# Routed expert results added to the output in DRAM by accumulating scatters

## The chip, the cores and the metric

The kernel runs on one core of a Trainium2 chip. A core has TensorE (PE, matrix products), VectorE (DVE), ScalarE (ACT), GpSimd (POOL) and SyncE (SP). Each has its own instruction queue, and they meet by semaphores. TensorE writes PSUM, here eight banks of 128 x 512 float32. DMA queues of SP, ACT and POOL feed the core's 16 DMA engines; the indirect ones, with a row index for each partition, are issued by GpSimd. The metric is the device time of one execution in microseconds (us), the median of several runs.

## What is computed

Eight blocks of 128 tokens, 512 wide, go through two layers with gated residuals. The change touches the last step alone, a mixture of experts added to x:

```python
# x = x + tanh(g_ffn[1]) * moe(layernorm(x))
logits = xt @ router_w + router_b
scores = softmax(logits) + router_bias
g = scores.reshape(T, GROUPS, E // GROUPS)              # 16 experts, 4 groups
_, gidx = top_k(g.max(axis=-1), LIM)                    # the 2 best groups
masked = where(keep[:, :, None], g, -inf).reshape(T, E)
_, idx = top_k(masked, K)                               # the 2 best experts
gate = zeros((T, E)).at[arange(T)[:, None], idx].add(vals)
for w1, b1, w2, b2, w3, b3, ge in experts:              # INTER = 128
    h = silu(xt @ w1 + b1) * (xt @ w2 + b2)
    y = y + ge[:, None] * (h @ w3 + b3)
z = silu(xt @ sw1 + sb1) * (xt @ sw2 + sb2) @ sw3 + sb3 # shared, 2 x 128
return y + z
```

T is 1024. Each token has two routed experts (TOP = 2), so there are 2048 token-expert pairs.

## The kernel before

The long part of the kernel, the two attention steps and the first feed-forward step, up to about 1100 us, is left as it is. Behind it come three pieces.

**The router and the shared experts.** VectorE works out the choice in many small steps (`router_shift`, `router_groups`, `router_choice`). TensorE multiplies the shared experts' weights in four pieces (`inner_part(n, 0)` and `(n, 1)`, n = 0 to 3; n = 0 and 1 are the first four token blocks, 2 and 3 the last four). Each piece then goes through ScalarE (`silu_of`), VectorE (`hidden`), ScalarE (`hidden_high`, the high half of a split float32) and GpSimd (`hidden_low`, the low half). `outer(t)` multiplies block t by the output weights, 7 matmuls into bank 4 or 5. ScalarE copies it out with the gate (`shared_rows`), GpSimd adds it to `x_sb` (`add_shared`), and from the third block on `outer` waits until the bank two blocks back has been copied.

**The sorting.** `rank_tokens` counts, by products with the 0/1 choice `chosen_b`, how many tokens go to each expert and which rank each has. VectorE turns this into tiles of 128 rows of one expert (`tile_ranges`, `places`): 31 tiles (TILES) hold the 2048 pairs, with empty places. `turn_selection` transposes the map from tiles to experts (`sel`, taken over into `sel_t`). `gather_tokens` gives every place its token number (`token_i`) by 16 products, and `load_offset` reads the address of each tile's weights.

**The loop over 31 tiles.** GpSimd gathers the tile's 128 token rows from DRAM (`gather(j)`, 256 KB, four buffers). TensorE transposes them (`turn_x_rows`), multiplies by w1 and w2 (`routed_inner`), transposes the hidden rows (`turn_hidden`) and multiplies by w3 (`routed_outer`, into bank 6 or 7). ScalarE copies the result to `y_rows`, two buffers (`take_y`), and SP stores it in `y_dram`. When all 31 are stored, GpSimd gathers 16 times 128 rows from `y_dram` back in token order (`y_back`), VectorE multiplies each by its gate and adds it to `x_sb` (`add_routed`), and SP stores the eight blocks of `out`.

The order on every queue is the order in which the functions are called in the code. In TensorE's loop it is

```python
for j in range(TILES):
    if j + 1 < TILES:
        routed_inner(j + 1)
    turn_hidden(j)
    if j + 2 < TILES:
        turn_x_rows(j + 2)
    routed_outer(j)
```

Of the kernel before, what the change touches and what calls it, by code (L numbers as in the profile page):

```python
# [18 lines left out]
F32 = mybir.dt.float32  # L19
# [35 lines left out]
def build(nc, x, ctx, ctx_t, g_xattn, g_ffn, wq, wkv, wo, q_w, k_w, w_gate, w_up, w_down, router_w, router_b,  # L55
          router_bias, s_w, s_b12, r_w, e_b, rows_dram, y_dram, out):
    with ExitStack() as top:
# [26 lines left out]
        slot_gates = sb("slot_gates", [P, TOP * NB])  # L84
        pos_row = sb("pos_row", [P, P])
# [8 lines left out]
        sel_t = sb("sel_t", [P, TL + 2], F32R)  # L94
        offset_i = sb("offset_i", [1, TL], I32)
        token_i = sb("token_i", [P, TL], U32)
        slot_i = sb("slot_i", [P, TOP * NB], U32)
# [68 lines left out]
        at[0] = gu_at - 2 * EW * 4  # L166
        y_back = put("y_back", [P, TOP * NB, D])
# [18 lines left out]
        at[0] = stage_at  # L186
        x_rows = put("x_rows", [P, 4, D])
        x_cols = put("x_cols", [P, 2, KC, P])
# [30 lines left out]
        dest, dest_tile, dest_pos = (put(n, [P, TOP * NB]) for n in ("dest", "dest_tile", "dest_pos"))  # L219
# [66 lines left out]
        y_loaded = [sem(f"y_loaded{i}") for i in range(PAIRS)]  # L286
        r_added = sem("r_added")
# [88 lines left out]

        block = top.enter_context(nc.Block())
# [3 lines left out]
        def _(sp):  # L381
# [103 lines left out]
        def _(pool):  # L485
# [6 lines left out]
            def routing_maps():  # L492
# [6 lines left out]
                          allow_small_or_imprecise_dtypes=True).then_inc(maps_ready, 1)  # L499
                pool.memset(ones_b[:, :], 1.0).then_inc(maps_ready, 1)  # L500
                pool.memset(chosen_b[:, NB, :], 0.0).then_inc(maps_ready, 1)
                pool.memset(tri[:, :, :], 1.0).then_inc(maps_ready, 1)
                pool.memset(sel[:, :], 0.0).then_inc(maps_ready, 1)
                pool.wait_ge(maps_ready, 7)
# [4 lines left out]
                for i, col in enumerate((E, 32 + E)):  # L509
                    pool.affine_select(out=sel[:, :], in_=sel[:, :], compare_op=ALU.not_equal, fill=1.0,  # L510
                                       base=-64 * TL - col, pattern=[[1, P]], channel_multiplier=64)\
                        .then_inc(maps_ready, 1)
                    pool.wait_ge(maps_ready, 10 + i)
# [181 lines left out]
        def _(act):  # L695
# [289 lines left out]
        def _(dve):  # L985
# [250 lines left out]
            chunks(dve, inner_chunk)  # L1236
            dve.wait_ge(bias_high, 1)
# [112 lines left out]
            def router_groups():  # L1350
# [7 lines left out]
                dve.wait_ge(maps_ready, 11)  # L1358
# [35 lines left out]
            def places():  # L1394
# [27 lines left out]
                dve.tensor_copy(slot_i[:, :], dest[:, :]).then_inc(places_ready, 1)  # L1422

            def take_selection():
                dve.wait_ge(sel_turned, 1)
                dve.tensor_copy(sel_t[:, :], bank[7][:, 0:TL + 2]).then_inc(sel_copied, 1)
# [7 lines left out]
            def gate_slots():  # L1434
# [5 lines left out]
                                       ALU.add))  # L1440

# [20 lines left out]
            def add_routed(c, t):  # L1462
                n = TOP * t + c
                dve.wait_ge(y_loaded[t // 2], 16 * 2 * TOP)
                dve.wait_ge(r_added, n) if c else dve.wait_ge(e_added, t + 1)
                dve.scalar_tensor_tensor(out=x_sb[:, t, :], in0=y_back[:, c * NB + t, :],
                                         scalar=slot_gates[:, c * NB + t:c * NB + t + 1], in1=x_sb[:, t, :],
                                         op0=ALU.mult, op1=ALU.add).then_inc(r_added, 1)


# [13 lines left out]
            gate_slots()  # L1484
            routed_hidden(0)
# [4 lines left out]
            for t in range(NB):  # L1490
                for c in range(TOP):
                    add_routed(c, t)
# [497 lines left out]
```

## Time and profile before

| | |
|---|---|
| median of 3 runs | 1299.7 us (1299.63 to 1300.89) |
| the profiled execution | 1297.4 us, its span 1295.2 us |
| busy, share of the span | PE 92%, DVE 63%, ACT 44%, POOL 26% |
| granted clock of TensorE | 0.975 of 2.4 GHz in the mean |

The span goes from the first to the last instruction of the core. Busy shares are means over stages with different limits: TensorE is busy nearly all the time until the routed loop ends, and idle behind it. A chain of waits follows the work that ended last back to what released it, step by step. "issue" in it is time in which the engine waited for nothing that the profile shows. A DMA's time "to landing" counts from the start of the instruction that issues it to its completion.

### The profile page before, as it was taken

What the parts mean: (1) busy time and instruction counts of PE and PEld (TensorE: products, weight loads), DVE (VectorE), ACT (ScalarE), POOL (GpSimd) and SP (SyncE); (2) the same over time, 40 slices, a digit from 0 to 9 for tenths busy, and PEclk for the clock granted to TensorE, in tenths of its full rate; (3) what the DMA queues carried; (4) which work ended last, traced back from release to release, by engine and by line L of the source; (5) the groups of instructions that cost most, each with busy time, mean ns of one, the idle gap of its engine ahead of it and who ended that gap; (6) DMA issues with size and microseconds to landing.
All of it is one profiled execution on the core that took longest, in us unless ns stands there. A gap on an engine that the chain in (4) does not pass through costs nothing.

```text
span 1295.2 us, 20292 instructions
## 1 busy us (share of the span) xinstructions
PE 1196.3 (92%) x6771; PEld 1015.7 (78%) x6771; DVE 818.3 (63%) x2402; ACT 575.4 (44%) x1345; POOL 340.7 (26%) x283
## 2 busy tenths in 40 slices
PE   5899999999999999999999999979999887899990
PEld 5788898888888888898889888857877664677760
DVE  6767667667666766766766766676878687611113
ACT  3545455454455454554555545433444323233430
POOL 4413023122121221321302312213432133252205
PEclk9999999999999999999999999989999998899995
DMA  7001001000000100100100000102213138134436
GB/s 260 1 34 49 2 34 50 1 32 16 32 32 2 47 32 0 49 0 32 49 0 32 0 1 1 52 1 77 65 57 100 65 98 320 70 113 138 141 109 199
DMA packets 39557, 77.41 MB, mean 60 GB/s; under 512 B 5266, under 2 KB 21650, under 8 KB 37460
## 3 DMA queue, kind: packets, MB, share of 16 engines
q1 hardware_dynamic: 34596, 62.36, 14.1%
q0 software_dynamic: 3760, 12.32, 3.6%
q10 hardware_dynamic: 1152, 2.10, 0.4%
q8 instruction: 28, 0.46, 0.2%
q14 instruction: 21, 0.17, 0.0%
HBM read 64.45 MB, written 12.32 MB: 59 GB/s over the span
## 4 chain that ended last, share of the span: by engine, by line
PE 54%; DVE 23%; issue 10%; ACT 6%; POOL 5%; DMA 1%; SPq 1%; DVEq 0%; POOLq 0%; ACTq 0%
PE bank L330 13%; PE bank L332 12%; PE bank L331 12%; PE bank L1838 4%; DVE iq L1232 2%; ACT probs L755 2%; PE bank L1586 2%; PE bank L1856 2%; DVE probs L1089 2%; DVE k_junk L1046 2%; PE bank L1722 2%; DVE row_max L1062 1%; DVE pt_lo L1076 1%; POOL k_rstd L540 1%; PE bank L1533 1%
## 5 line engine op out<-in xcount | busy, mean ns | idle before, releaser
L755 ACT ACTIVATE probs<-bank,exp_bias,q_rstd 128x256 f32<-128x256 f32 x256 | 141.2, 562 | 142.8 <-DVE exp_bias L1070 142.8
L1081 DVE TENSOR_TENSOR o_lo<-bank,o_hi 128x512 fp32r<-128x512 f32 x64 | 44.2, 691 | 186.3 <-ACT o_hi L748 186.2
L330 PE MATMUL bank<-wkv_hi,kv_src_lo 128*128 128x256 f32 x512 | 146.2, 286 | 3.0 <-POOL wkv_lo L522 3.0
L332 PE MATMUL bank<-wkv_hi,kv_src_hi 128*128 128x256 f32 x512 | 146.0, 285 | 0.0
L331 PE MATMUL bank<-wkv_lo,kv_src_hi 128*128 128x256 f32 x512 | 145.8, 285 | 0.0
L544 POOL TENSOR_TENSOR q_rstd<-q_var,minus_half 128x8 f32<-128x8 f32 x32 | 52.4, 1638 | 304.3 <-DVE q_var L1049 304.3
L744 ACT ACTIVATE pt_hi<-bank 128x512 fp32r<-128x512 f32 x128 | 69.7, 597 | 115.9 <-PE bank L1586 115.9
L330 PE MATMUL bank<-wo_hi,o_lo 128*128 128x512 f32 x256 | 105.4, 412 | 1.0 <-DVE o_lo L1081 1.0
L330 PE MATMUL bank<-wq_hi,kv_src_lo 128*128 128x512 f32 x256 | 103.2, 403 | 0.0
L330 PEld LDWEIGHTS bank<-wkv_hi,kv_src_lo 128*128 128x128 f32 x512 | 98.6, 193 | 4.7 <-issue 3.4
L332 PE MATMUL bank<-wo_hi,o_hi 128*128 128x512 f32 x256 | 102.1, 399 | 0.0
L331 PE MATMUL bank<-wo_lo,o_hi 128*128 128x512 f32 x256 | 101.9, 398 | 0.0
L332 PE MATMUL bank<-wq_hi,kv_src_hi 128*128 128x512 f32 x256 | 100.6, 393 | 0.0
L331 PE MATMUL bank<-wq_lo,kv_src_hi 128*128 128x512 f32 x256 | 100.3, 392 | 0.0
L331 PEld LDWEIGHTS bank<-wkv_lo,kv_src_hi 128*128 128x128 f32 x512 | 98.7, 193 | 1.4
L332 PEld LDWEIGHTS bank<-wkv_hi,kv_src_hi 128*128 128x128 f32 x512 | 98.7, 193 | 0.0
L540 POOL TENSOR_TENSOR k_rstd<-k_var,minus_half 128x4 f32<-128x4 f32 x32 | 32.5, 1016 | 248.6 <-DVE k_var L1023 248.6
L1062 DVE TENSOR_REDUCE row_max<-bank 128x2 f32<-128x512 f32 x128 | 84.7, 684 | 18.4 <-PE bank L332 17.6
L1089 DVE TENSOR_SCALAR probs<-probs,row_inv 128x256 f32<-128x256 f32 x256 | 88.0, 407 | 2.2
L330 PE MATMUL bank<-k_hi,q_lo 128*128 128x256 f32 x256 | 78.3, 306 | 6.6 <-DVE q_lo L1055 5.4
L1076 DVE TENSOR_TENSOR pt_lo<-bank,pt_hi 128x512 fp32r<-128x512 f32 x128 | 81.7, 679 | 0.0
L331 PE MATMUL bank<-k_lo,q_hi 128*128 128x256 f32 x256 | 73.1, 286 | 0.0
(256 smaller groups left out, 3089.2 us busy)
## 6 DMA issues: line engine op xcount, KB each, us to landing
weights<-r_w SPq DMA_DIRECT2D x16, 768.0 KB, 8.8
wq_raw<-wq SPq DMA_DIRECT2D x8, 1024.0 KB, 4.8
wo_raw<-wo SPq DMA_DIRECT2D x8, 1024.0 KB, 4.8
y_dram<-y_rows SPq DMA_DIRECT2D x31, 256.0 KB
wkv_raw<-wkv SPq DMA_DIRECT2D x8, 512.0 KB, 3.3
gu_raw<-w_gate SPq DMA_DIRECT2D x10, 256.0 KB, 3.3
gu_raw<-w_up SPq DMA_DIRECT2D x10, 256.0 KB, 3.7
wd_raw<-w_down SPq DMA_DIRECT2D x10, 256.0 KB, 4.0
```

Source lines behind the costliest of these rows:

```text
L330: eng.matmul(out_ap, a_lo, b_hi, start=start, stop=False)
L331: eng.matmul(out_ap, a_hi, b_lo, start=False, stop=False)
L332: return eng.matmul(out_ap, a_hi, b_hi, start=False, stop=stop)
L540: pool.tensor_tensor(k_rstd[:, :], k_var[:, :], minus_half[:, 0:4], ALU.pow).then_inc(k_rstd_ready, 1)
L544: pool.tensor_tensor(q_rstd[:, par, :], q_var[:, :], minus_half[:, 0:2 * R], ALU.pow)\
L744: act.activation(pt_hi[:, c, :], pt_ps[c][:, :], ACT.Copy).then_inc(pt_hi_ready, 1)
L755: act.activation(probs[:, h, :], scores_ps[h // 2][:, (h % 2) * 256:(h % 2) * 256 + 256], ACT.Exp, bias=exp_bias[:, h:h + 1], scale=q_rstd ...
L1062: dve.tensor_reduce(row_max[:, 2 * half:2 * half + 2], scores_ps[half][:, :].rearrange("p (h n) -> p h n", h=2), AX.X, ALU.max)\
L1076: dve.tensor_tensor(pt_lo[:, c, :], pt_ps[c][:, :], pt_hi[:, c, :].bitcast(F32), ALU.subtract)\
L1081: dve.tensor_tensor(o_lo[:, par, :], o_ps[:, :], o_hi[:, par, :].bitcast(F32), ALU.subtract)\
L1089: dve.tensor_scalar(probs[:, h, :], probs[:, h, :], row_inv[:, h:h + 1], None, ALU.mult)\
L1838: mm = pe.matmul(bank[j % 2][:, 0:2 * P], x_cols[:, j % 2, k, :], weights[:, bass.ds(at_weights[j] + k * 2 * P, 2 * P)], start=False, stop ...
```

## The change

`y_dram`, `y_back`, `slot_i`, the 16 gathers and the 16 adds are gone. Instead:

- SP stores block t of `out` as soon as the shared part has been added to it. A ninth block is stored too; it takes the rows of empty places, and is cut off on the host.
- `take_y` scales each result row by the gate of its place (`place_gates`).
- GpSimd adds the tile's 128 rows to the rows of `out` in DRAM by an indirect DMA with `compute_op=ADD` (`scatter(j)`), once the nine stores have landed. Each scatter waits until the one before has landed. The gathers from tile 4 on are issued in between.
- The output row and the gate of each place (`place_i`, `place_gates`) come from 16 further products (`gather_late`) of 96 columns, prepared by VectorE (`gate_slots`) and taken over by `take_late`.
- The bias selector of the shared part is a tensor of its own (`shared_sel`), so `outer` needs no `sel_t`. `outer(0)` to `outer(3)` move ahead of `rank_tokens`; `outer(6)` and `outer(7)` move between the offset loads and the loop. ScalarE's and GpSimd's queues are reordered to match.
- `x_rows` and `x_cols` move to the start of the shared memory region, where `xt_hi` was.

```diff
@@ sync @@
-            for j in range(TILES):
-                sp.wait_ge(y_rows_ready, j + 1)
-                sp.dma_start(y_dram[j * P:j * P + P, :], y_rows[:, j % 2, :]).then_inc(y_stored[j % 2], 16)
             for t in range(NB):
-                sp.wait_ge(r_added, TOP * (t + 1))
+                sp.wait_ge(e_added, t + 1)
                 sp.dma_start(out[t, :, :], x_sb[:, t, :]).then_inc(stored, 16)
-            sp.wait_ge(stored, 16 * NB)
+            sp.dma_start(out[NB, :, :], x_sb[:, 0, :]).then_inc(stored, 16)
+            sp.wait_ge(stored, 16 * (NB + 1))
+            for i in range(2):
+                sp.wait_ge(y_stored[i], 16 * ((TILES + 1 - i) // 2))
@@ gpsimd @@
-            add_shared(0)
-            add_shared(1)
+            for t in range(4):
+                add_shared(t)
             hidden_low(3)
-            add_shared(2)
-            add_shared(3)
             pool.wait_ge(tokens_ready, 1)
...
+            def scatter(j):
+                pool.wait_ge(y_rows_ready, j + 1)
+                if j >= 1:
+                    pool.wait_ge(y_stored[(j - 1) % 2], 16 * ((j + 1) // 2))
+                pool.indirect_dma_start(out_rows, bass.IndirectOffsetOnAxis(ap=place_i[:, j:j + 1], axis=0),
+                                        y_rows[:, j % 2, :], None, compute_op=ALU.add).then_inc(y_stored[j % 2], 16)
+
             for j in range(4):
                 gather(j)
             for t in range(4, NB):
                 add_shared(t)
-            for j in range(4, TILES):
-                pool.wait_ge(x_rows_turned, j - 3)
-                gather(j)
-            for i in range(2):
-                pool.wait_ge(y_stored[i], 16 * ((TILES + 1 - i) // 2))
-            for t in range(NB):
-                for c in range(TOP):
-                    q = c * NB + t
-                    pool.indirect_dma_start(y_back[:, q, :], None, y_dram[:, :],
-                                            bass.IndirectOffsetOnAxis(ap=slot_i[:, q:q + 1], axis=0))\
-                        .then_inc(y_loaded[t // 2], 16)
+            pool.wait_ge(late_taken, 2)
+            pool.wait_ge(stored, 16 * (NB + 1))
+            for j in range(TILES):
+                if j + 4 < TILES:
+                    pool.wait_ge(x_rows_turned, j + 1)
+                    gather(j + 4)
+                scatter(j)
@@ scalar @@
-            shared_rows(0)
-            shared_rows(1)
+            for t in range(4):
+                shared_rows(t)
             silu_of(3)
             hidden_high(3)
-            for t in range(2, NB):
+            for t in range(4, NB - 1):
                 shared_rows(t)
...
                     act.wait_ge(e_added, NB)
-                act.activation(y_rows[:, j % 2, :], bank[6 + j % 2][:, :], ACT.Copy).then_inc(y_rows_ready, 1)
+                    act.wait_ge(late_taken, 2)
+                act.activation(y_rows[:, j % 2, :], bank[6 + j % 2][:, :], ACT.Copy, scale=place_gates[:, j:j + 1])\
+                   .then_inc(y_rows_ready, 1)
 
             take_x_cols(0)
+            shared_rows(NB - 1)
             take_x_cols(1)
@@ vector @@
-                dve.tensor_copy(slot_i[:, :], dest[:, :]).then_inc(places_ready, 1)
...
+                step(dve.tensor_copy(gates_hi[:, :], slot_gates[:, :]))
+                step(dve.tensor_tensor(gates_lo[:, :], slot_gates[:, :], gates_hi[:, :].bitcast(F32), ALU.subtract))
...
+                for i, value in enumerate((place[:, :], gates_hi[:, :].bitcast(F32), gates_lo[:, :].bitcast(F32))):
+                    dve.tensor_tensor(at_late[:, :, i * TL:i * TL + TL], at_tile[:, :, :],
+                                      value.unsqueeze(2).broadcast_to([P, TOP * NB, TL]), ALU.mult).then_inc(late_ready, 1)
...
-            for t in range(NB):
-                for c in range(TOP):
-                    add_routed(c, t)
@@ tensor @@
+            def gather_late():
+
+                pe.wait_ge(late_ready, 3)
+                for q in range(TOP * NB):
+                    mm = pe.matmul(bank[7][:, 128:128 + 3 * TL], at_pos[:, q, :], at_late[:, q, :], start=(q == 0),
+                                   stop=(q == TOP * NB - 1))
+                mm.then_inc(late_done, 1)
...
+            pe.wait_ge(shared_sel_ready, 1)
+            for t in range(4):
+                outer(t)
             rank_tokens()
             inner_part(3, 0)
             inner_part(3, 1)
             turn_selection()
-            pe.wait_ge(sel_copied, 1)
-            outer(0)
-            outer(1)
-            outer(2)
-            outer(3)
             gather_tokens()
-            for t in range(4, NB):
-                outer(t)
+            outer(4)
+            outer(5)
             pe.wait_ge(offset_ready, 1)
...
+            outer(6)
+            turn_x_rows(0)
+            outer(7)
+            gather_late()
+            turn_x_rows(1)
             pe.wait_ge(weights_loaded, 16 * E)
-            turn_x_rows(0)
-            turn_x_rows(1)
             routed_inner(0)
```

GpSimd's queue, the end of it, before: the shared additions, the gathers of the loop, then those behind it.

```order
L660 TENSOR_TENSOR x_sb<-s_rows,x_sb 128x512 [waits e_rows_ready] x2
L673 DMA x_rows<-rows_dram,token_i 128x512 [waits rows_stored1,rows_stored0,tokens_ready]
L673 DMA x_rows<-rows_dram,token_i 128x512 x3
L660 TENSOR_TENSOR x_sb<-s_rows,x_sb 128x512 [waits e_rows_ready] x4
L673 DMA x_rows<-rows_dram,token_i 128x512 [waits x_rows_turned] x27
L689 DMA y_back<-y_dram,slot_i 128x512 [waits y_stored1,y_stored0]
L689 DMA y_back<-y_dram,slot_i 128x512 x15
```

And now:

```order
L667 TENSOR_TENSOR h_lo<-e_h,h_hi 128x512 [waits h_hi_ready]
L683 DMA x_rows<-rows_dram,token_i 128x512 [waits rows_stored1,rows_stored0,tokens_ready]
L683 DMA x_rows<-rows_dram,token_i 128x512 x3
L672 TENSOR_TENSOR x_sb<-s_rows,x_sb 128x512 [waits e_rows_ready] x4
L683 DMA x_rows<-rows_dram,token_i 128x512 [waits x_rows_turned,stored,late_taken]
L691 DMA out<-y_rows,place_i 1152x512 [waits y_rows_ready]
L683 DMA x_rows<-rows_dram,token_i 128x512 [waits x_rows_turned]
L691 DMA out<-y_rows,place_i 1152x512 [waits y_stored0,y_rows_ready]
```

The last two rows repeat, with `y_stored1` and `y_stored0` in turn: a gather stands ahead of each scatter, 27 of them, and the last four scatters follow one another. The gather of tile 4 now stands behind the wait for the nine stores.

TensorE's queue around the rank product (operands `chosen_b`), before: the end of the third inner piece, the rank product, the start of the fourth inner piece.

```order
L332 MATMUL bank<-xt_hi,e_hi 128x512
L1795 MATMUL bank<-chosen_b,before_t 128x144 [waits chosen_ready,bias_split,logits_ready]
L1798 MATMUL bank<-chosen_b,ones_b 128x128
L1798 MATMUL bank<-chosen_b,ones_b 128x112
L1798 MATMUL bank<-chosen_b,ones_b 128x96
```

And now, from the end of the third inner piece, with the rows of `outer(0)` and then the end of `outer(3)`:

```order
L339 MATMUL bank<-xt_hi,e_hi 128x512
L337 MATMUL bank<-e_hi,h_lo 128x512 [waits e_lo_ready,shared_sel_ready,h_lo_ready,bias_split,logits_ready]
L338 MATMUL bank<-e_lo,h_hi 128x512
L339 MATMUL bank<-e_hi,h_hi 128x512
...
L1813 MATMUL bank<-bias_t,shared_sel 128x512
L1820 MATMUL bank<-chosen_b,before_t 128x144 [waits chosen_ready]
L1823 MATMUL bank<-chosen_b,ones_b 128x128
```

Four outer products, 28 matmuls, have moved from behind the transposed selection to ahead of the rank product.

## Rows read from the trace of the kernel before

**Rows 1.** The page: the span.

```profile
span 1295.2 us, 20292 instructions
```

**Rows 2.** Windows by stage: length, busy time (instructions) of each engine, clock, DMA share, GB/s.

```profile
core 0: us, PE busy (x) PEld busy (x) DVE busy (x) ACT busy (x) POOL busy (x), PEclk, DMA share, GB/s
1112.90:1117.80 4.90, 0.04 (x2) 0.06 (x2) 4.49 (x14) 1.97 (x3) 1.26 (x1) 0.92 0.00 0
1117.80:1123.60 5.80, 5.80 (x21) 4.70 (x22) 4.55 (x15) 0.63 (x1) 1.52 (x1) 0.50 0.00 0
...
1146.30:1261.00 114.70, 113.93 (x519) 83.49 (x519) 15.31 (x62) 44.28 (x91) 26.69 (x28) 1.00 0.42 130
```

**Rows 3.** Chain of waits, one tile: start us, us, what.

```profile
1150.24 0.11 PE bank L1848
...
1153.93 0.11 PE bank L1848
```

**Rows 4.** Chain of waits, after the last tile.

```profile
1261.07 0.61 ACT y_rows L971
...
1261.69 2.03 DMA y_dram<-y_rows
1263.71 0.26 issue
1263.97 0.95 POOL y_back L689
1264.92 0.30 issue
...
1283.94 5.62 DMA y_back<-y_dram,slot_i
...
1291.96 0.75 DVE x_sb L1466
```

**Rows 5.** Tile x_rows, gathers of the loop: duration ns min/median/max, time to landing.

```profile
L673 POOL DMA_INDIRECT x_rows<-rows_dram,token_i x25: 945/947/957, 1151.1 to 1239.7; - x25
...
DMA to landing us min/median/max: 3.5/4.2/4.8
```

**Rows 6.** Tile y_back, the gathers behind the loop.

```profile
DMA to landing us min/median/max: 3.4/4.1/5.6
```

**Rows 7.** Tile out, plain stores of 256 KB.

```profile
DMA to landing us min/median/max: 2.0/3.7/4.4
```

**Rows 8.** DMA queues, 1264 to 1290 us: packets, MB, share of 16 engines.

```profile
q0 software_dynamic: 1280, 4.20, 58.0%
```

**Rows 9.** Timeline of GpSimd (POOL): start us, us, instruction, idle time before it.

```profile
1112.98 1.26 POOL L655 TENSOR_TENSOR h_lo<-e_h,h_hi 128x512 fp32r<-128x512 f32 x1 [9.07 <-ACT h_hi L885]
...
1137.50 1.20 POOL L673 DMA_INDIRECT x_rows<-rows_dram,token_i  x1 [0.18 <-issue]
...
1147.56 0.97 POOL L673 DMA_INDIRECT x_rows<-rows_dram,token_i  x1 [0.16 <-issue]
```

**Rows 10.** Timeline of TensorE (PE).

```profile
1117.77 0.28 PE L1795 MATMUL bank<-chosen_b,before_t 128*128 128x144 bf16 x1 [4.86 <-DVE chosen_b L1376]
...
1127.20 0.50 PE L330 MATMUL bank<-e_hi,h_lo 128*128 128x512 f32 x1 [0.35 <-DVE sel_t L1426]
...
1133.75 1.85 PE L1814 MATMUL bank<-at_token,at_pos 128*128 128x32 f32 x16
```

**Rows 11.** Timeline of ScalarE (ACT).

```profile
1118.32 0.63 ACT L885 ACTIVATE h_hi<-e_h 128x512 fp32r<-128x512 f32 x1 [3.42 <-DVE e_h L1446]
...
1152.13 0.60 ACT L971 ACTIVATE y_rows<-bank 128x512 f32<-128x512 f32 x1 [0.71 <-issue]
```

**Rows 12.** Timeline of VectorE (DVE).

```profile
1126.95 0.19 DVE L1426 CAST sel_t<-bank 128x34 fp32r<-128x34 f32 x1 [3.94 <-PE bank L1805]
...
1130.82 1.27 DVE L1422 CAST slot_i<-dest 128x16 uint32<-128x16 f32 x1
...
1135.64 0.19 DVE L1430 CAST token_i<-bank 128x32 uint32<-128x32 f32 x1 [2.85 <-PE bank L1814]
```

More of the change, by code:

```diff
@@ L55, in build @@
 def build(nc, x, ctx, ctx_t, g_xattn, g_ffn, wq, wkv, wo, q_w, k_w, w_gate, w_up, w_down, router_w, router_b,
-          router_bias, s_w, s_b12, r_w, e_b, rows_dram, y_dram, out):
+          router_bias, s_w, s_b12, r_w, e_b, rows_dram, out):
     with ExitStack() as top:
@@ L165, in build @@
         weights = put("weights", [P, E * EW])
-        at[0] = gu_at - 2 * EW * 4
-        y_back = put("y_back", [P, TOP * NB, D])
+        at[0] = start
+        x_rows = put("x_rows", [P, 4, D])
+        x_cols = put("x_cols", [P, 2, KC, P])
+        at_late = put("at_late", [P, TOP * NB, 3 * TL], F32R)
         at[0] = stage_at
@@ L218, in build @@
         tiles_before = put("tiles_before", [P, E, E])
-        dest, dest_tile, dest_pos = (put(n, [P, TOP * NB]) for n in ("dest", "dest_tile", "dest_pos"))
+        dest, dest_tile, dest_pos, place = (put(n, [P, TOP * NB]) for n in ("dest", "dest_tile", "dest_pos", "place"))
         at[0] = e_h_at
@@ L285, in build @@
         y_stored = [sem(f"y_stored{i}") for i in range(2)]
-        y_loaded = [sem(f"y_loaded{i}") for i in range(PAIRS)]
-        r_added = sem("r_added")
+        late_ready, late_done, late_taken = sem("late_ready"), sem("late_done"), sem("late_taken")
+        shared_sel_ready = sem("shared_sel_ready")
         gu_hi_ready = sem("gu_hi_ready")
@@ L375, in chunks @@
             one_chunk(CH - 1, 0, TAIL, 0)
+        out_rows = out.rearrange("a p n -> (a p) n")
         block = top.enter_context(nc.Block())
@@ L508, in routing_maps @@
                                    pattern=[[1, E], [-1, E]], channel_multiplier=0).then_inc(maps_ready, 1)
[L509 to L513, printed above, removed]
+                for i, row in enumerate((E, 32 + E)):
+                    pool.affine_select(out=shared_f[:, :], in_=shared_f[:, :], compare_op=ALU.not_equal, fill=1.0,
+                                       base=-row, pattern=[[0, 1]], channel_multiplier=1).then_inc(maps_ready, 1)
+                    pool.wait_ge(maps_ready, 13 + i)
             def ln_root(i, s=0):
@@ L1440, in gate_slots, with take_late @@
                                        ALU.add))
+                step(dve.tensor_copy(gates_hi[:, :], slot_gates[:, :]))
+                step(dve.tensor_tensor(gates_lo[:, :], slot_gates[:, :], gates_hi[:, :].bitcast(F32), ALU.subtract))
+                step(dve.scalar_tensor_tensor(out=place[:, :].rearrange("p (c t) -> p c t", c=TOP),
+                                              in0=dest_pos[:, :].rearrange("p (c t) -> p c t", c=TOP), scalar=-1.0,
+                                              in1=token_less[:, :].unsqueeze(1).broadcast_to([P, TOP, NB]), op0=ALU.mult,
+                                              op1=ALU.add))
+                dve.wait_ge(h_done, 4 * SHARED)
+                for i, value in enumerate((place[:, :], gates_hi[:, :].bitcast(F32), gates_lo[:, :].bitcast(F32))):
+                    dve.tensor_tensor(at_late[:, :, i * TL:i * TL + TL], at_tile[:, :, :],
+                                      value.unsqueeze(2).broadcast_to([P, TOP * NB, TL]), ALU.mult).then_inc(late_ready, 1)
+            def take_late():
+                dve.wait_ge(late_done, 1)
+                dve.tensor_scalar(place_i[:, :], bank[7][:, 128:128 + TL], past_rows[:, 0:1], None, ALU.add)\
+                    .then_inc(late_taken, 1)
+                dve.tensor_copy(gates_taken[:, :], bank[7][:, 128 + TL:128 + 2 * TL]).then_inc(late_ready, 1)
+                dve.wait_ge(late_ready, 4)
+                dve.tensor_tensor(place_gates[:, :], bank[7][:, 128 + 2 * TL:128 + 3 * TL], gates_taken[:, :], ALU.add)\
+                    .then_inc(late_taken, 1)
             def hidden(n):
@@ L1804, in turn_selection @@
                 pe.wait_ge(sel_ready, 2)
-                pe.transpose(bank[7][:, 0:TL + 2], sel[0:TL + 2, :], ident[0:TL + 2, 0:TL + 2])\
+                pe.transpose(bank[7][:, 0:TL], sel[0:TL, :], ident[0:TL, 0:TL])\
                     .then_inc(sel_turned, 1)
@@ L1983 @@
             for k, v in arrays.items()}
-    out = nc.dram_tensor("out", (NB, P, D), F32, kind="ExternalOutput").ap()
+    out = nc.dram_tensor("out", (NB + 1, P, D), F32, kind="ExternalOutput").ap()
     rows_dram = nc.dram_tensor("rows_dram", (NB * P, D), F32, kind="Internal").ap()
-    y_dram = nc.dram_tensor("y_dram", (TILES * P, D), F32, kind="Internal").ap()
-    build(nc, rows_dram=rows_dram, y_dram=y_dram, out=out, **args)
+    build(nc, rows_dram=rows_dram, out=out, **args)
     r = run_bass_kernel_spmd(nc, [arrays], core_ids=[0])
-    return r.results[0]["out"]
+    return r.results[0]["out"][:NB]
```

40 lines of the change are left out of this document (24 added, 16 removed).

## The prediction

> **What bounds the kernel now.** I read four views. First the page for the span, 1295.2 us [rows 1]. Then the windows and the chain of waits of the routed stage. From 1146.3 to 1261.0 TensorE is busy 113.93 of 114.70 us at the full clock of 2.4 GHz [rows 2], and one tile's step follows the next after 3.69 us (1150.24 to 1153.93) [rows 3], so this loop of 31 tiles is bound by TensorE. Third the chain behind it [rows 4]: the last y_rows copy ends at 1261.68, its store lands 2.03 us later, GpSimd wakes 0.26 us after that, issues 16 gathers one behind the other (0.95 us each with 0.30 between most of them), the last one lands 5.62 us after its start, and VectorE's last add ends at 1292.71. The store that follows takes 2.0 us [rows 7] and the span ends 0.5 us behind it. So 33.5 us lie behind the last copy, in which TensorE does nothing. Fourth, the timelines ahead of the loop, for the moved outer products.
>
> **What the change takes away.** The whole tail: the last store to y_dram, 16 gathers, 16 adds and 8 stores of out. With the tail gone and nothing put in its place the span would end near 1262.
>
> **What it adds, the term that decides.** Each tile's 128 result rows are now added to the output in DRAM by an accumulating scatter from GpSimd's queue, and scatter j waits until scatter j-1 has landed. Neither y_rows (two buffers) nor PSUM (two banks) lets TensorE run more than a few tiles ahead. So if a scatter's cycle S is longer than TensorE's 3.69 us, the loop runs at S, and the scatters are the chain. S = wake of GpSimd + L, where L is the time from the start of the scatter's issue to its landing. The wake is 0.26 us [rows 4]. No row shows an accumulating DMA, so L is bounded from rows.
>
> - Below: the quickest gather of the same 128 rows of 2 KB by the same queue landed 3.4 us after its start [rows 6]. The scatter also reads 128 scattered rows from DRAM, and writes to DRAM too, so I find no reason for less.
> - Above: a gather of the loop, 4.2 us at the median [rows 5], followed by a whole store of 256 KB, 2.0 us at the least [rows 7], the two not overlapping: 6.2 us.
> - Taken: the loop's gather, 4.2 us, which has its issue of 0.95 us in it and shares the engines with one other transfer per tile, as the scatter will (the gather of tile j+5 takes the place of the y_dram store). To it comes the moving of a second 256 KB, since the destination rows and the rows of y_rows are both read. What one gather occupies is 58.0% of 26 us over 16 gathers = 0.94 us [rows 8]. L = 4.2 + 0.94 = 5.14 us and S = 5.40 us. This is nearer to the middle than to an end; I keep both ends.
>
> In the trace a gather moves its bytes once, and 0.94 us is that share. The Trainium skill, Collectives: The Full Stack, section The bandwidth ceiling, says that a reducing transfer is slower because it needs two source reads on one read ring, and not because of the addition. No run here shows it; by that rule the second 0.94 us is right and the sum stands, and without it L would be 4.2 us and the sum 1296.
>
> The gather of tile j+5 is issued inside the flight of scatter j: 0.95 us of issue [rows 5] out of L less the scatter's own issue, about 4.2 us, so it costs nothing as long as L is over 2.5 us. The scaling by the gate rides on the copy that was there (0.60 us [rows 11]) and costs nothing.
>
> **Where the first scatter starts.** It needs y_rows of tile 0, written until 1152.73 [rows 11], and all nine stores of out. The pieces ahead of the loop, one by one:
>
> - Outer products 0 to 3 move ahead of the rank product. That product waited 4.86 us for VectorE's choice and began at 1117.77 [rows 10]. Four outer products took 1127.20 to 1133.75, 6.55 us, or 1.6 each [rows 10]. Outer 0 can begin when the low half of block 1 is there, 1112.98 + 1.26 = 1114.24 [rows 9], and outer 1 ends at 1117.5. But outer 2 waits until ScalarE has emptied bank 4, and ScalarE does that only behind the copy of 1118.32 to 1118.95 [rows 11], plus 0.69: 1119.6. Outer 3 ends at 1122.9. So the rank product, with VectorE's tile ranges and places queued behind it, is late by about 5.1 us.
> - It gets back part: before, the clock fell to 1.2 GHz behind the idle 4.9 us, 0.50 from 1117.8 to 1123.6 [rows 2]. If it does not fall, the 5.8 us at the half level become 2.9. The transposed selection then comes at about 1126.95 - 0.2 + 5.1 - 2.9 = 1129. From there to the last at_pos was 1130.9 - 1126.95 = 4.0 us, and the 1.27 us cast to slot_i behind it is gone [rows 12]: 1133. TensorE has nothing to do in between, so gather_tokens ends right behind, about 1134.4, not at 1135.6, and token_i comes about 1 us earlier than 1135.64 [rows 12]. The first gather moves from 1137.50 [rows 9] to about 1136.5.
> - That 1 us is spent again: outer 7 (1.6 us) and 16 small products for the late places (1.85 us for the 16 like them [rows 10], perhaps a little more with 96 columns in place of 32) now stand between the two transposes of x_rows. Routed work begins at about 1146.3 as before, give or take 1.5 us. VectorE's new casts and products (some 3 us) end near 1140, under outer products.
> - The nine stores of out: the last shared add ends near 1146.5 and a store lands in 2.0 to 4.4 us [rows 7], so by 1151. Queued behind that wait on GpSimd is the gather of tile 4, which left at 1147.56 [rows 9]; leaving at 1151 it lands at 1155.2, and its transpose is due three steps after 1146.3 + 3.9, near 1157.5. Covered; without that cover it would cost the difference once.
>
> So the first scatter starts at 1152.73 + 0.26 = 1153.0.
>
> **The sum.** Last landing = 1153.0 + 31 S - 0.26; the span ends 0.5 us later: 1153.2 + 31 x 5.40 = 1320.6. Against 1295.2 this is +25.4 us: the loop's 31 tiles cost 31 x (5.40 - 3.69) = 53.0 us more, the tail of 33.5 us shrinks to the last scatter's 5.9. The profiled execution took 1297.4 us, so 1322.8 for it; the median of the runs, 1299.7, is 2.3 above that, and 1299.7 + 25.4 = 1325.
>
> **The point of balance.** The span stays at 1295.2 when S = (1295.2 - 1153.2) / 31 = 4.58, that is L = 4.32 us. The median gather, 4.2, is just below it. Everything hangs on how much an accumulating scatter takes more than a gather.
>
> **Rivals.**
>
> 1. Faster: the second read and the write overlap the first, row by row. For it speaks that a plain store lands in 2.0 us [rows 7], so writing to DRAM has no long receipt, and that quiet gathers took 3.4. At L = 4.2 the sum is 1291.5, or 1296 by the median; at L = 3.4, S is 3.66, TensorE bounds the loop, and the span ends at 1261.7 + 0.26 + 3.4 + 0.5 = 1265.8, 29.4 less: 1270. Against it: the same bytes can't be moved twice in the time of once, and the loop's gathers were at 4.2 and not 3.4 because of their neighbour. It decides below L = 4.24. Chance 0.15. Part of it is a page's rule: the Trainium skill, DMA: Bandwidth & Descriptors, section Anatomy of one DMA, gives 2.0 us plus bytes over 436 GB/s for a DMA of this queue, an estimate of 2.6 us for 256 KB. TensorE would bound the loop by that rule too, at 1270; the trace's quickest gather, 3.4 us, disagrees, and I give that end 0.03 of the 0.15.
> 2. No change: L between 4.24 and 4.41, by chance. 0.05.
> 3. Dearer: read, add and write of a row stand one behind another, or the issue is longer for the added descriptors. At L = 6.2 the sum is 1153.2 + 31 x 6.46 = 1353.5, or 1358; beyond that 0.07.
> 4. The clock: TensorE is busy 3.69 of 5.40 us, and it fell to the half level once behind 4.9 us of idling [rows 2]. If it stayed low, a tile would need up to 2 x 3.69 = 7.4 us and TensorE would bound the loop: 1153.2 + 31 x 7.4 = 1382.6, or 1387. Against it: idle pieces here are 1.7 us, and when it is the bound it is busy throughout, in which state the clock came back within 5.8 us [rows 2]. 0.03.
>
> **How the numbers follow.** The forecast, L from 4.41 to 6.2 (1302 to 1358), has 0.70. Faster by over 0.2% (2.6 us, about what can be told from no change here) 0.15, same 0.05, slower 0.80. The range goes from 1290 (L = 4.0, a little of rival 1) to 1360 and leaves out about 0.2.
>
> **What would show it.** Right: scatters follow each other at 5.4 us, each gap on GpSimd ended by the previous scatter's landing, landing 5.1 us after issue; TensorE's share in the loop near 0.7; the rank product 3 to 6 us later, the first y_rows within 1.5 us of 1152.7; the end one landing behind the last scatter. Wrong: a pace of 3.7 us with TensorE full, a landing under 4.3 us, or a granted clock near 0.5 in the loop.

## Result and the profile after

The changed kernel takes 1334.6 us in the median of 4 runs (1334.1 to 1336.0) against 1299.9 us before, a ratio of 1.0269 with a 95% interval of 1.0255 to 1.0283. Timed a second time beside the experiments below it stood at 1.0256 (1.0232 to 1.0279). The profiled execution took 1334.5 us, its span 1332.8 us. The forecast was 1325 us, slower, in a range of 1290 to 1360 us.

The windows of the loop and its end, with the columns of [rows 2]:

```profile
core 0: us, PE busy (x) PEld busy (x) DVE busy (x) ACT busy (x) POOL busy (x), PEclk, DMA share, GB/s
...
1200.00:1250.00 50.00, 36.70 (x147) 25.91 (x146) 4.47 (x16) 12.36 (x26) 21.82 (x18) 0.90 0.53 95
...
1310.00:1333.00 23.00, 3.04 (x8) 1.11 (x7) 0.87 (x3) 2.23 (x4) 6.25 (x4) 0.64 0.34 46
```

TensorE was busy 113.93 of 114.70 us in the loop before [rows 2]; now it is busy 36.70 of 50, a share of 0.73. The chain of waits over the first scatters (start us, us, what) is a chain of landings, where [rows 3] was one of matrix products:

```profile
1158.65 4.90 DMA out<-y_rows,place_i
...
1163.60 0.75 issue
1164.35 4.77 DMA out<-y_rows,place_i
1169.16 0.05 issue
1169.20 0.70 ACT y_rows L985
1169.91 4.95 DMA out<-y_rows,place_i
...
1174.95 0.70 ACT y_rows L985
...
1175.78 4.69 DMA out<-y_rows,place_i
```

The instructions of the tile `out` (duration ns min/median/max, first and last start us, then the time to landing) and of the gathers in the same loop, to be set beside [rows 5, 6]:

```profile
L691 POOL DMA_INDIRECT out<-y_rows,place_i x31: 1550/1587/1643, 1158.7 to 1327.7; - x31
...
DMA to landing us min/median/max: 4.4/4.8/5.7
```

```profile
L683 POOL DMA_INDIRECT x_rows<-rows_dram,token_i x27: 963/990/1004, 1155.5 to 1301.9; - x27
...
DMA to landing us min/median/max: 3.4/4.4/4.8
```

From the first start, 1158.65, to the last, 1327.66, the 30 cycles take 5.63 us each. A scatter lands 4.8 us after its start; the other 0.8 us is GpSimd's way from that landing to the next start. The gathers' own issue is nearly unchanged, 0.99 us, and a scatter's is 1.59 us.

One reading needs care. The timeline of GpSimd names ScalarE's copy as what released most scatters:

```profile
1164.35 1.59 POOL L691 DMA_INDIRECT out<-y_rows,place_i  x1 [2.75 <-DMA out<-y_rows,place_i]
...
1169.91 1.58 POOL L691 DMA_INDIRECT out<-y_rows,place_i  x1 [2.68 <-ACT y_rows L985]
...
1175.78 1.60 POOL L691 DMA_INDIRECT out<-y_rows,place_i  x1 [2.99 <-ACT y_rows L985]
```

```profile
1165.07 0.69 ACT L985 ACTIVATE y_rows<-bank,place_gates 128x512 f32<-128x512 f32 x1 [0.71 <-PE bank L1891]
...
1169.20 0.69 ACT L985 ACTIVATE y_rows<-bank,place_gates 128x512 f32<-128x512 f32 x1 [1.15 <-DMA out<-y_rows,place_i]
```

The scatter at 1169.91 sends the third tile's rows, which were copied from 1165.07 on and had been ready since 1165.8. The copy at 1169.20 is the fourth tile's; it was itself released by the landing at 1169.1 of the scatter that used its buffer. Both hang on the same landing, and the profile names the one that ended later. The chain's "0.70 ACT y_rows" between two landings is therefore not a price of ScalarE; the first pair, 1163.56 to 1164.35 (the 0.75 us of issue), shows the same gap with no copy in it. From the second scatter on, each one's rows had been copied 2.3 us or more before it started.

### The profile page after: what moved, and what is told of

It reads as the page before. It is cut to its first block, busy times and chain, and to the rows that moved or that the text cites. A ratio compares the mean times of both kernels' runs of the same rounds, so it can differ in the third digit from the quotient of the medians.

```text
span 1332.8 us, 20323 instructions
## 1 busy us (share of the span) xinstructions
PE 1212.3 (91%) x6787; PEld 1024.8 (77%) x6787; DVE 811.7 (61%) x2395; ACT 575.9 (43%) x1345; POOL 374.1 (28%) x301
## 4 chain that ended last, share of the span: by engine, by line
PE 46%; DVE 22%; DMA 12%; issue 10%; ACT 7%; POOL 3%; SPq 1%; DVEq 0%; POOLq 0%; ACTq 0%
PE bank L337 13%; PE bank L339 13%; PE bank L338 12%; DMA out<-y_rows,place_i 11%; DVE iq L1248 2%; ACT probs L768 2%; PE bank L1611 2%; DVE probs L1105 2%; DVE k_junk L1062 2%; PE bank L1747 2%; ACT y_rows L985 1%; DVE row_max L1078 1%; DVE pt_lo L1092 1%; POOL k_rstd L552 1%; PE bank L1558 1%
## 5 line engine op out<-in xcount | busy, mean ns | idle before, releaser
L552 POOL TENSOR_TENSOR k_rstd<-k_var,minus_half 128x4 f32<-128x4 f32 x32 | 32.5, 1016 | 247.9 <-DVE k_var L1039 247.9
L1496 DVE COPY g_ht<-bank 128x128 f32<-128x128 f32 x31 | 9.0, 292 | 119.2 <-PE bank L1881 119.2
```

The lines of the kernel that those rows point to most:

```text
L552: pool.tensor_tensor(k_rstd[:, :], k_var[:, :], minus_half[:, 0:4], ALU.pow).then_inc(k_rstd_ready, 1)
```

## Experiments

Each rests on the profile of one execution unless an interval stands beside it. The second trace of the kernel before belongs first, since it says which differences between two traces mean anything.

**The kernel before once more.**

> The kernel before, unchanged, for a second trace. The changed kernel's choice (chosen_b) came 4.0 us later than in the first trace of before, and in its variants 1.9 to 4.6 us later. If that is spread between executions, this trace has its choice anywhere from 1117 to 1122 us and its span moves with it, 1293 to 1299 us. If it is the change (rival), it stands at 1117.3 us within 0.5 again.

Its span and its choice, and below them the choice in the changed kernel:

```profile
span 1299.0 us, 20292 instructions
```

```profile
1121.77 0.29 DVE L1376 TENSOR_TENSOR chosen_b<-r_pick 128x128 bf16<-128x128 f32 x1
```

```profile
1121.36 0.29 DVE L1394 TENSOR_TENSOR chosen_b<-r_pick 128x128 bf16<-128x128 f32 x1
```

The same kernel has its choice at 1121.77, 4.4 us later than in the first trace (1117.3), and a span of 1299.0 in place of 1295.2 us. The changed kernel stands at 1121.36. The second trace of the changed kernel has it at 1119.6. So the 4.0 us by which all of the changed kernel's routed part is late against the first trace lie within the spread between executions of one kernel, and need no cause in the change. Seven timed executions of the kernel before went from 1298.5 to 1302.6 us. From here on I count from the choice. That leaves a smaller spread: the first y_rows copy starts 34.8 us after the choice in the first trace of the kernel before and 35.4 us after it in the second.

**The addition left out.**

```diff
-  y_rows[:, j % 2, :], None, compute_op=ALU.add).then_inc(y_stored[j % 2], 16)
+  y_rows[:, j % 2, :], None).then_inc(y_stored[j % 2], 16)
```

> The scatters write the rows instead of adding them (the addition into the output is left out), still one at a time. Theory A: the addition is paid where the scatter is issued (1.59 us of issue against 0.95 for a gather, and a longer start-up ahead of it, 0.77 against 0.3), so without it issue falls to about 0.95 us, landing to 3.0 to 3.4 us, the cycle goes under 3.7 us, TensorE bounds the loop again and the span is about 1273 us. Rival B: it is the indexed write to DRAM that is dear and the addition is free in the stream: issue stays near 1.6 us, the cycle at 5.2 to 5.6 us, the span at 1320 to 1333 us.

```profile
span 1271.4 us, 20323 instructions
```

```profile
L691 POOL DMA_INDIRECT out<-y_rows,place_i x31: 969/987/1009, 1156.6 to 1267.9; - x31
```

```profile
1264.27 2.69 DMA out<-y_rows,place_i
...
1266.99 0.02 POOLq L690
1267.01 0.70 issue
```

```profile
core 0: us, PE busy (x) PEld busy (x) DVE busy (x) ACT busy (x) POOL busy (x), PEclk, DMA share, GB/s
...
1190.00:1260.00 70.00, 70.00 (x323) 51.19 (x322) 9.26 (x38) 29.49 (x57) 35.29 (x36) 1.00 0.42 139
```

The same 31 indexed writes, one at a time, issue in 0.99 us and land 2.7 us after their start, and TensorE is busy 70.00 of 70 us again. The trace shows a landing only where a scatter waited for it, six times; five were at 2.7 to 2.8 us and one at 3.8. The time is 1273.1 us, the span 1271.4 against 1332.8. Theory A holds for the cost as a whole: index and DRAM are cheap, the addition (with its read of the old row, which no run takes apart from it) is what costs, 0.6 us of it at issue and 1.5 us (3.2 less 1.7 us behind the issue) in flight. Its second half falls: the 0.7 us and more between a landing and the next start is there for the plain scatter too, 0.79 to 1.09 us in those six starts (the last from 1266.97 to 1267.93). The other scatters started 0.27 us and more after ScalarE's copy.

**Half the columns, and half the rows.**

```diff
-  pool.indirect_dma_start(out_rows, ...place_i[:, j:j + 1]..., y_rows[:, j % 2, :], ...
+  pool.indirect_dma_start(half, ...place_i[:, j:j + 1]..., y_rows[:, j % 2, 0:D // 2], ...   # e2
+  pool.indirect_dma_start(out_rows, ...place_i[0:P // 2, j:j + 1]..., y_rows[0:P // 2, j % 2, :], ...   # e7
```

> The scatters add only the first 256 of 512 columns, into a DRAM buffer of their own (the other half of each row is left out), 128 rows each as before. Prediction's term (the second read moves its bytes in 0.94 us, so half the bytes save about 0.9 us of both reads): landing falls from 4.8 to about 3.9 us, cycle to 4.7 us, span near 1305 us. Theory A (issue by rows, flight mostly latency): issue stays at 1.59 us, landing 4.4 to 4.7 us, cycle 5.2 to 5.5 us, span 1319 to 1330 us.

> The scatters add only the first 64 of the 128 rows of each tile, all 512 columns (the other rows are left out). Half the bytes, as with half the columns, and half the rows. If the issue goes by rows: issue falls from 1.59 to 0.9 to 1.1 us and landing to 3.1 to 3.4 us (3.8 less the saved issue), cycle about 4.1 us, span 1285 to 1292 us. If the issue is a fixed cost of adding: issue stays at 1.59, landing 3.8 us as with half the columns, cycle 4.65 us, span near 1304 us.

The first run writes to a DRAM buffer of its own, with nine more stores ahead of the first scatter, which so starts late (1161.3). Rows of the first, then of the second:

```profile
L693 POOL DMA_INDIRECT half<-y_rows,place_i x31: 1549/1586/1644, 1161.3 to 1298.8; - x31
...
DMA to landing us min/median/max: 3.5/3.8/4.1
```

```profile
L691 POOL DMA_INDIRECT out<-y_rows,place_i x31: 1405/1441/1502, 1158.3 to 1293.8; - x31
...
DMA to landing us min/median/max: 3.4/3.7/4.8
```

Half the bytes take 1.0 to 1.1 us off the landing, in both shapes: 3.8 and 3.7 in place of 4.8 us. The prediction's term holds (half the bytes were to save 0.9 us), and its number for the first run, landing 3.9 and span 1305, met 3.8 and 1303.4. The issue hardly goes by rows, 1.44 us for 64 and 1.59 for 128; with a cycle of 4.52 us and a span of 1298.2 the half rows lie nearer to a fixed issue (4.65 us) than to one by rows (4.1 us), and match neither. An estimate, if the bytes count in proportion, takes an accumulating scatter of 256 KB apart: 1.59 us issue, some 1.2 us that depend on nothing tried here, and 2.0 us for the bytes, where 0.94 us was a gather's share [rows 8].

**Nothing beside the scatters.**

```diff
             for j in range(TILES):
-                if j + 4 < TILES:
-                    pool.wait_ge(x_rows_turned, j + 1)
-                    gather(j + 4)
                 scatter(j)
```

> As the changed kernel, but the gathers from tile 4 on are left out (the tiles reuse the first four tiles' rows), so that no other transfer runs beside a scatter. Prediction's step (0.7 to 0.8 us of the 4.2 us gather was its neighbour, 3.4 without one): landing falls from 4.8 to 4.0 to 4.2 us, cycle from 5.63 to 4.9 us, span near 1311 us. Rival (the scatter's time is its own): landing 4.7 to 4.8 us, cycle 5.5 us, span 1327 to 1333 us.

```profile
L691 POOL DMA_INDIRECT out<-y_rows,place_i x31: 1553/1557/1638, 1157.8 to 1323.8; - x31
...
DMA to landing us min/median/max: 4.4/4.7/5.9
```

Landing 4.7 against 4.8 us, cycle 5.53 against 5.63 us, span 1328.7. The rival holds: the scatter's time is its own, and a gather beside it costs 0.1 us.

With the scatters alone in the loop, the DMA engines' share gives a second measure of their bytes (columns as in [rows 2]):

```profile
1190.00:1260.00 70.00, 50.28 (x211) 33.99 (x211) 7.25 (x25) 17.45 (x39) 20.24 (x13) 0.98 0.35 45
```

A share of 0.35 in cycles of 5.53 us is 1.9 us of all 16 engines for each accumulating scatter, near the 2.0 us estimated from half the bytes. A plain scatter comes to 0.6 us by the same reckoning (0.42 of 3.69 us, less the gather's 0.94).

**Two chains.**

```diff
-                if j >= 1:
-                    pool.wait_ge(y_stored[(j - 1) % 2], 16 * ((j + 1) // 2))
-                pool.indirect_dma_start(out_rows, ...
+                if j >= 2:
+                    pool.wait_ge(y_stored[j % 2], 16 * (j // 2))
+                pool.indirect_dma_start(out_rows[j % 2], ...
```

> Even tiles are added to one DRAM buffer and odd tiles to another, so that two scatters may be in flight; the sum of both buffers is left out. If the one-at-a-time wait is the whole cost: the pace falls to TensorE's 3.7 us or to GpSimd's own work per tile (0.3 + 1.0 for the gather, 0.8 + 1.6 for the scatter, 3.7 us), and the span is 1275 to 1285 us. If the scatters slow one another in the DMA engines (rival: contention): landing goes over 6 us and the pace stays over 4.5 us, span over 1300 us.

```profile
span 1277.6 us, 20331 instructions
```

```profile
1214.62 1.59 POOL L693 DMA_INDIRECT out<-y_rows,place_i  x1 [0.80 <-ACT y_rows L987]
...
1218.30 1.59 POOL L693 DMA_INDIRECT out_b<-y_rows,place_i  x1 [0.81 <-ACT y_rows L987]
...
1222.12 1.59 POOL L693 DMA_INDIRECT out<-y_rows,place_i  x1 [0.94 <-ACT y_rows L987]
```

```profile
1190.00:1260.00 70.00, 70.00 (x324) 51.74 (x323) 9.15 (x39) 29.64 (x57) 48.88 (x39) 1.00 0.79 143
```

With two scatters in flight the pace is 3.7 us, TensorE is busy 70.00 of 70 us and the span is 1277.6 us, although nine more stores ahead of the loop hold the first scatter until 1164.1. The additions themselves go on as before, with an issue of 1.59 us each; their landings do not show in this trace. So neither GpSimd's work nor the DMA engines (share 0.79) held the loop; the wait for the scatter before did.

**The outer products put back.**

```diff
             pe.wait_ge(shared_sel_ready, 1)
-            for t in range(4):
-                outer(t)
             rank_tokens()
             inner_part(3, 0)
             inner_part(3, 1)
             turn_selection()
+            for t in range(4):
+                outer(t)
             gather_tokens()
```

(`shared_rows` and `add_shared` follow on their queues as in the kernel before.)

> As the changed kernel, but the first four shared outer products stand behind the transposed selection again. My step: the rank product comes about 5.3 us earlier relative to the choice, the tokens about 1 us later, and the first scatter moves by under 2 us either way, span 1331 to 1335 us. Rival: the move is what made the start late (the changed kernel's first scatter comes 5.6 us after that of the old timing), then the span falls by 4 to 5 us to about 1328.

> The changed kernel, unchanged, timed on the same chip as the next three. Its ratio to before should stand at 1.0255 to 1.0283 again.

> The changed kernel with the four outer products behind the selection again, now timed. The traces gave 3.5 us from the choice to the first scatter for the move. If that is its price: 3 to 4 us (0.25%) under the changed kernel of the same call, ratio to before 1.023 to 1.025. Rival (it was the spread between executions): within 1 us of the changed kernel.

Windows of the changed kernel, its rank product and the products of `gather_tokens`, and then the same two rows with the outer products back:

```profile
core 0: us, PE busy (x) PEld busy (x) DVE busy (x) ACT busy (x) POOL busy (x), PEclk, DMA share, GB/s
...
1133.30:1136.00 2.70, 0.03 (x1) 0.06 (x1) 2.62 (x5) 0.00 (x0) 0.00 (x0) 0.94 0.64 203
1136.00:1146.20 10.20, 9.87 (x33) 8.37 (x34) 5.84 (x14) 1.32 (x2) 6.38 (x6) 0.51 0.92 283
```

```profile
1126.95 0.24 PE L1820 MATMUL bank<-chosen_b,before_t 128*128 128x144 bf16 x1
...
1135.97 3.57 PE L1839 MATMUL bank<-at_token,at_pos 128*128 128x32 f32 x16 [2.74 <-DVE at_pos L1437]
```

```profile
1121.16 0.22 PE L1822 MATMUL bank<-chosen_b,before_t 128*128 128x144 bf16 x1 [4.86 <-DVE chosen_b L1396]
...
1135.48 1.85 PE L1841 MATMUL bank<-at_token,at_pos 128*128 128x32 f32 x16
```

The move costs. From the choice to the first scatter are 37.3 us in the changed kernel and 33.8 us here. Timed, 1333.0 us against 1329.8 us, ratios to before 1.0256 (1.0232 to 1.0279) and 1.0221 (1.0201 to 1.0241). The difference of 3.2 us is near the 3.5 of the traces. The two intervals overlap, but the times themselves do not: 1332.4 to 1336.1 us against 1329.0 to 1330.6. The second pair of traces repeated it: from the choice to the first y_rows copy 36.3 and 32.6 us, as in the first pair. My expectation (under 2 us) was wrong, and so was the rival's size. Where it comes from is in the rows. Ahead of the rank product the four outer products fill the 4.86 us in which TensorE waited for the choice, and run 5.2 us over. Behind the selection they no longer fill the time in which VectorE makes at_pos, and there TensorE now waits 2.74 us with nothing to do. Then the 16 products of `gather_tokens` take 3.57 us in place of 1.85, since the granted clock is 0.51 from 1136 to 1146.2, that is 1.2 of 2.4 GHz, with outer products 4 and 5 in it. Every trace with all four ahead (seven) has the wait of 2.74 us and the 3.57 us (3.56 in one); none of the traces with them behind has either. The tokens gained nothing: the first gather leaves 18.8 us after the choice in both kernels.

**A version that beats both.** Each gated row is written, not added, by the plain scatter, to a row of its own for token and choice, so no store of `out` has to land ahead of the loop; behind it come contiguous loads, 16 adds and the stores. The outer products stand behind the selection.

```diff
-  y_rows[:, j % 2, :], None, compute_op=ALU.add).then_inc(y_stored[j % 2], 16)
+  y_rows[:, j % 2, :], None).then_inc(y_stored[j % 2], 16)      # into y_tok, 17 blocks of 128 rows
...
+            for t in range(NB):                                    # sync
+                sp.dma_start(y_back[:, t, :], y_tok[t, :, :]).then_inc(y_loaded[t], 16)
+            for t in range(NB):                                    # scalar
+                act.dma_start(y_back[:, NB + t, :], y_tok[NB + 1 + t, :, :]).then_inc(y_loaded[t], 16)
+                    dve.tensor_tensor(x_sb[:, t, :], y_back[:, c * NB + t, :], x_sb[:, t, :], ALU.add)
```

> A version meant to beat both: each gated row is written, not added, by a plain scatter to a row of its own (choice, token) in a DRAM buffer, one scatter at a time; behind the loop 16 contiguous loads on the SP and ACT queues, 16 adds on VectorE and 8 stores of out; the first four outer products stand behind the selection. From the plain scatter (landing about 2.7 us, hidden under TensorE's 3.7 us): the loop ends with its last scatter landing near 1266 us; then 4 MB of loads at 300 to 400 GB/s take 10 to 14 us with the adds under way, the last two adds and a store 4 us: span 1281 to 1287 us, 1284 to 1291 us by the clock of the runs, 0.7 to 1.2% under before. Rival: the loads slow one another and the stores, and the end takes over 30 us as before: within 0.3% of before.

> The version with token-ordered plain scatters again, beside the next one: ratio to before 0.990 to 0.994.

1291.2 and 1291.6 us, ratios 0.9922 (0.9903 to 0.9941) and 0.9924 (0.9903 to 0.9946). The end after the last y_rows copy is 24.9 us here (1265.0 to 1289.9), not the 33.5 of [rows 4]. The last scatter landed at 1269.9 where the expectation had 1266, partly because this execution's choice was as late as 1121.8. From there the end took 20.0 us. The expectation was over-optimistic on the loads: they took 14.2 us (10 to 14 expected), the last of 16 landed 10.6 us after its start with the DMA engines full, and 5.8 us were left behind it, not 4.

```profile
1264.31 0.69 ACT L991 ACTIVATE y_rows<-bank,place_gates 128x512 f32<-128x512 f32 x1 [1.16 <-PE bank L1906]
```

```profile
1267.14 2.75 DMA y_tok<-y_rows,place_i
...
1273.50 10.62 DMA y_back<-y_tok
...
1284.94 0.69 DVE x_sb L1532
```

**Two outer products ahead, two behind.**

```diff
             pe.wait_ge(shared_sel_ready, 1)
+            outer(0)
+            outer(1)
             rank_tokens()
             inner_part(3, 0)
             inner_part(3, 1)
             turn_selection()
-            for t in range(4):
-                outer(t)
+            outer(2)
+            outer(3)
             gather_tokens()
```

> As v1, but outer products 0 and 1, which need nothing that comes late, stand ahead of the rank product, and 2 and 3 behind the selection. They fit into the 4.9 us in which TensorE waited for the choice, so the rank product is not late, the clock does not fall ahead of the fourth inner piece (2.9 us back at the selection), and TensorE still has two outer products while VectorE makes at_pos. First scatter 1.5 to 3 us earlier after the choice than in v1, time 1.5 to 3 us under v1. Rival: the tokens wait for VectorE's places anyway, or the clock falls at another place: within 1 us of v1.

```profile
1120.08 0.24 PE L1835 MATMUL bank<-chosen_b,before_t 128*128 128x144 bf16 x1
...
1129.77 1.04 PE L1854 MATMUL bank<-at_token,at_pos 128*128 128x32 f32 x8
1131.14 1.06 PE L1854 MATMUL bank<-at_token,at_pos 128*128 128x32 f32 x8 [0.34 <-DVE at_pos L1447]
```

```profile
core 0: us, PE busy (x) PEld busy (x) DVE busy (x) ACT busy (x) POOL busy (x), PEclk, DMA share, GB/s
1118.00:1124.00 6.00, 6.00 (x35) 4.78 (x34) 5.61 (x14) 2.28 (x4) 2.59 (x3) 1.00 0.01 3
1124.00:1130.00 6.00, 6.00 (x28) 4.44 (x26) 5.74 (x14) 0.20 (x1) 1.20 (x1) 1.00 0.45 156
```

1287.5 us against 1291.6, timed beside it, 4.0 us less where 1.5 to 3 were expected; the ratio to before is 0.9901 (0.9880 to 0.9922). The rank product starts 0.4 us after the choice as it does in the kernel before, the clock stays at 1.00 through the fourth inner piece, and TensorE waits 0.34 us for at_pos, not 2.74. The first y_rows copy comes 30.7 us after the choice (32.5 and 33.5 in the two traces of the version with all four behind), so 1.9 to 2.9 us of the 4.0 are the move's by the traces; the rest lies mostly ahead of the choice, where executions differ anyway. This is the fastest of the kernels run.

## Why the prediction was right, and where it was off

**The decision and its sign: right.** The chain is made of landings, TensorE has time to spare, and the scatter's landing lies above the balance of 4.32 us. That the wait for the scatter before is the cause is shown by the two chains, that it is the addition (with its read) by the plain scatter.

**L, the landing: 5.14 forecast, 4.8 measured, from parts that were mis-sized against each other.** The size of the second pass over the bytes was right: 1.9 to 2.0 us for 256 KB against a gather's 0.94. The base was not. I took the loop's median gather with 4.2 us, and held that 0.8 of it was the neighbour. Without a neighbour a scatter lands at 4.7, so it loses 0.1 to one; the changed kernel's gathers, beside a scatter, are at 4.4 at the median in one trace and at 4.1 in the other. The issue, which I took from the gathers at 0.95 us, is 1.59 us. And what the gather has besides issue and bytes, 4.2 - 0.95 - 0.94 = 2.3 us, is some 1.2 us for the scatter. The plain scatter makes it plainer: without the addition it lands at 2.7 us, 1.5 under my base, and the addition costs 2.1 us, not 0.94. These misses run against each other, so that 5.14 came near 4.8 is in part luck.

**The wake: 0.26 forecast, 0.8 measured.** This is the term that put the sum off most: 0.55 us in each of 31 cycles, 17 us, against which the shorter landing stands with 0.34 x 31 = 11 us. [Rows 4] shows GpSimd waking after a landing on SP's queue. After a landing on its own queue it takes 0.75 us and more, with the addition or without. It is not the scatter as such: the first one starts 0.27 us behind ScalarE's copy (1158.38 to 1158.65). I had no row of that case and put no bound on it. Why it takes longer was not tested. S came to 5.63 in place of 5.40 us, and the stage of the scatters to 174.2 (1158.65 to 1332.8) in place of 167.6 us.

**The start of the first scatter: 1153.0 forecast, 1158.65 measured.** Of these 5.65 us, 4.0 lie ahead of the choice, where two traces of the kernel before differ by 4.4. From the choice on it was 37.3 us in place of 35.7, 1.6 us late, just outside the 1.5 I allowed; measured from the second trace of the kernel before it would be 0.7 us less. Step by step: the rank product was to be late by 5.1 us and was by 5.2 (1126.95 against 1117.77, less 4.0); the selection by 2.2 and was by 2.4; the first gather was to be 1.0 us early and was 1.35 early (1140.15 against 1137.50, less 4.0), though not by the move of the outer products, without which it leaves as early. The step that failed is the next one. I wrote that TensorE has nothing to do while at_pos is made, and let the clock come back at the rank product, but did not ask what the new idle time of 2.74 us does to the clock: the products behind it ran at half of it for 10 us. What the move costs by itself, 3.5 us, was partly hidden in the sum by what the rest of the change saves in that stretch.

**Hidden costs.** The gathers, the gate's scaling (0.69 in place of 0.60 us a copy), the nine stores and the late gather of tile 4 cost nothing that shows. The gather of tile 4 left at 1155.49, and its transpose at 1163.13 did not wait for it.

**Together.** 1332.8 = 1295.2 + 25.4 forecast + 6.6 for the cycle + 5.65 for the start. By the medians the change costs less, 34.7 us against 37.6 by the two spans, mostly since the first trace of the kernel before lay 2.3 us under its median.

**The rivals.** The quick landing (0.15) did not come. The Trainium skill, DMA: Bandwidth & Descriptors, section Anatomy of one DMA, gives 2.0 us plus bytes over 436 GB/s for a DMA of this queue, an estimate of 2.6 us for 256 KB. The plain scatter's 2.7 us agrees with it; the accumulating one's 4.8 us does not, nor do the gathers of the loop (3.4 us at the quickest). The Trainium skill, Collectives: The Full Stack, section The bandwidth ceiling, puts the price of a reducing transfer on its second read and not on the addition. The 1.9 to 2.0 us of the bytes against 0.94 fit that, but no run here parts the read from the addition, and the 0.6 us of added issue are no matter of the bytes. The clock did fall in the loop at times, 0.90 in the mean from 1200 to 1250 and 0.58 from 1176 to 1180, and it moved no scatter: their rows were ready 2.3 us or more ahead.

## What to carry to other kernels

Here each accumulating scatter waits for the one before, because two tiles may add to the same row of `out`; no run tried it without that wait on one target. Where one waits so, the loop pays a whole round trip for each tile: price the round trip as issue plus flight plus the issuing engine's wake, against the pace of the loop, before counting what the tail saves. Where every row can have a place of its own, a plain scatter does the same sorting in the loop at no cost that shows, and the addition can be done in order behind it. Work moved into one idle stretch of TensorE is taken from another: of four pieces behind the selection, moving two ahead filled both gaps and gained 4 us, moving all four lost 3.

## What the runs showed of the hardware

- An accumulating indirect DMA of 128 rows of 2 KB lands 4.8 us after its start, a plain one 2.7 us. Half the bytes take 1.0 us off; a gather beside it costs 0.1 us. It occupies all 16 DMA engines for 1.9 us, an estimate from their share (0.35 of 5.53 us).
- Its issue on GpSimd takes 1.59 us for 128 rows and 1.44 us for 64, a plain scatter's 0.99 us.
- From a landing on GpSimd's own queue to the next indirect DMA that waited for it pass 0.75 to 0.94 us in the changed kernel and 0.79 to 1.09 us with plain scatters, from a landing on SP's queue 0.26 us (one case), from the end of ScalarE's copy 0.27 us.
- An idle stretch of 2.74 us of TensorE was followed by 10 us at a granted clock of 0.51. In the loop, idle stretches of up to 2.9 us left the mean at 0.90 and more, with falls of a few us between (0.58 from 1176 to 1180). So the length of a stretch alone does not tell what the clock does.
- One and the same kernel reached its choice at 1117.3 in one execution and at 1121.8 us in another.
